# A three-round slot-attention and FFN kernel: the loop over the rounds written out as straight code

## The reference

```
k = ln(ctx) @ wk + bk;  v = ln(ctx) @ wv + bv
slots = q_mu + exp(q_logsig) * layernorm(x)
for _ in range(3):
    q      = ln(slots) @ wq + bq
    attn   = softmax(k @ q.T / scale, over slots) + 1e-8
    attn   = attn / attn.sum(over tokens)
    slots  = (attn.T @ v) @ wu + bu + slots
    slots  = gelu(ln(slots) @ w1 + b1) @ w2 + b2 + slots
    slots  = ln(slots + cond)
x = x + slots
h = layernorm(gelu(layernorm(x) @ ternary(W_fc).T)) * w + b
x = x + h @ ternary(W_proj).T
```

## Time and profile before

| | |
|---|---|
| runs, median of 3 | 343.67 us (343.62 to 344.61) |
| profiled execution | 340.61 us |
| its span | 338.7 us, mean granted TensorE clock 0.995 |
| PE busy | 316.1 us (93%) |
| DVE busy | 294.2 us (87%) |
| ACT busy | 235.9 us (70%) |
| POOL busy | 202.7 us (60%) |

### The profile page before, as it was taken

How to read it: one execution, slowest core, us unless ns; L and a number is a source line. 1 busy time by engine, 2 the same in 40 slices (tenths; PEclk the granted TensorE clock), 3 DMA queues, 4 the chain that set the end, 5 groups by cost and what they waited for, 6 DMA issues and landing times. The chain is left out here.

```text
span 338.7 us, 6940 instructions
## 1 busy us (share of the span) xinstructions
PE 316.1 (93%) x1758; PEld 260.4 (77%) x1758; DVE 294.2 (87%) x851; ACT 235.9 (70%) x563; POOL 202.7 (60%) x385
## 2 busy tenths in 40 slices
PE   8999999999999899799999899799969799999995
PEld 7887888888887778688877788587846577777774
DVE  3699968898899989699999898989898999999874
ACT  2369986968458867386678675656537888888881
POOL 3268965256698763557887636556753965444341
PEclk9999999999999999999999999999998999999999
DMA  7997000000000000000000000000000000000001
GB/s 284 329 344 319 0 1 2 0 0 4 0 2 1 0 3 1 3 1 0 0 1 0 0 0 1 2 0 2 1 0 0 3 31 35 31 29 2 34 31 62
DMA packets 5310, 13.19 MB, mean 39 GB/s; under 512 B 672, under 2 KB 672, under 8 KB 4896
## 3 DMA queue, kind: packets, MB, share of 16 engines
q1 hardware_dynamic: 4160, 10.88, 8.7%
q10 hardware_dynamic: 1120, 1.98, 1.6%
HBM read 10.76 MB, written 2.10 MB: 38 GB/s over the span
## 5 line engine op out<-in xcount | busy, mean ns | idle before, releaser
L293 DVE BATCH_NORM_STATS2 stats<-S 128x6 f32<-128x256 f32 (+1 forms) x112 | 42.1, 417 | 9.4 <-DMA S<-ctx 3.5
L344 PE MATMUL ps_mid<-XT,KT 128*128 128x256 f32 x192 | 46.1, 383 | 3.9 <-ACT XT L360 3.9
L344 PE MATMUL ps_low<-V,PR 128*128 128x257 f32 x192 | 46.4, 384 | 3.5 <-DVE PR L866 3.5
L344 PE MATMUL ps_low<-wn,GT 128*128 128x256 f32 x192 | 46.4, 385 | 1.1 <-ACT GT L642 1.1
L344 PE MATMUL ps_mid<-XT,wt 128*128 128x256 f32 x192 | 45.6, 380 | 0.7 <-ACT XT L360 0.7
L344 PEld LDWEIGHTS ps_low<-V,PR 128*128 128x128 f32 x192 | 35.8, 190 | 10.8 <-DVE PR L866 3.8
L639 ACT ACTIVATE PR<-ps_mid,nmax 128x256 f32<-128x256 f32 x48 | 22.4, 472 | 30.1 <-DVE nmax L876 30.0
L344 PEld LDWEIGHTS ps_low<-wn,GT 128*128 128x128 f32 x192 | 36.8, 194 | 7.1 <-ACT GT L642 2.1
L311 POOL TENSOR_TENSOR lnm_ab<-lnm_mv,mhalf 128x2 f32<-128x2 f32 x24 | 17.3, 721 | 41.5 <-DVE lnm_mv L301 41.5
L344 PEld LDWEIGHTS ps_mid<-XT,KT 128*128 128x128 f32 x192 | 34.6, 190 | 8.9 <-ACT PR L639 4.6
L360 ACT ACTIVATE XT<-ps_t 128x512 f32<-128x512 f32 x56 | 33.2, 592 | 8.6 <-PE ps_t L336 8.6
(11 more groups left out here) (124 smaller groups left out, 704.1 us busy)
## 6 DMA issues: line engine op xcount, KB each, us to landing
S<-ctx SPq DMA_DIRECT2D x8, 256.0 KB, 3.8
X<-x SPq DMA_DIRECT2D x8, 256.0 KB, 3.4
out<-X SPq DMA_DIRECT2D x8, 256.0 KB, 2.0
rowv<-rows SPq DMA_DIRECT2D x1, 1920.0 KB, 9.6
wf<-w_fc_t SPq DMA_DIRECT2D x1, 1024.0 KB, 11.5
wf<-w_proj_t SPq DMA_DIRECT2D x1, 1024.0 KB, 13.5
wt<-w_tr ACTq DMA_DIRECT2D x1, 512.0 KB, 4.3
wn<-w_nat ACTq DMA_DIRECT2D x1, 512.0 KB, 5.4
```

Of the source, the lines that this page charges most:

```text
L293: dve.bn_stats(ln.st[:, at, j, 0:6], tiles[:, j]).then_inc(ln.stats_done, 1)
L344: last = pe.matmul(dst(m), lhs_t[:, c, m * P:(m + 1) * P], rhs[:, c, 0:n], start=(c == 0), stop=(c == 1))
```

## The change

`in_rounds` no longer makes a loop. It calls the step function for t = 0 and t = 1 as plain numbers, so steps 7 to 22 stand twice in each engine's program, with constant semaphore counts and constant addresses. The tests that told the written-out head by `isinstance(t, int)` now ask for `t == 0` (on DVE together with `s < LEAD`). The order of the steps and the operations in them are unchanged, as are the loops of the prologue and of the FFN. The diff, cut:

```diff
-        def in_rounds(eng, step):
+        def in_rounds(step):
             for s in range(LEAD):
                 step(0, s, False)
-            with eng.Fori(0, ROUNDS - 1) as t:
+            for t in range(ROUNDS - 1):
                 for s in range(LEAD, STEPS + LEAD):
                     step(t, s, False)
             for s in range(LEAD, STEPS + LEAD):
...
-                if isinstance(t, int) and not last and s < 2:
+                if t == 0 and not last and s < 2:
                     ln_coef(pool, lni, B - 2 + s, s)
...
-                head = isinstance(t, int) and not last
+                head = t == 0 and s < LEAD and not last
...
-                chunk = None
+                part = None
                 if not head and not last and s < LEAD + B:
-                    k = s - LEAD
-                    chunk = (t * B + k) * CHUNK
-                    chunk_slot[0] = k % 2
-                    cut = bass.ds(chunk, CHUNK)
+                    part = t * B + (s - LEAD)
+                    cut = slice(part * CHUNK, (part + 1) * CHUNK)
...
             def ternary_below(n, cut):
-                dve.tensor_scalar(below[:, chunk_slot[0]], wf[:, cut], thr_now(1, n), None, ALU.is_lt).then_inc(below_ready, 1)
+                dve.tensor_scalar(below[:, n % 2], wf[:, cut], thr[:, 1, n // B:n // B + 1], None, ALU.is_lt)\
+                   .then_inc(below_ready, 1)
...
-            in_rounds(dve, rounds_with_pass)
+            in_rounds(rounds)
```

More of the change, by code:

```diff
@@ L457, in rounds @@
             def rounds(t, s, last):
-                if s == 2 and isinstance(t, int) and not last:
+                if s == 2 and t == 0 and not last:
                     pool.wait_ge(rows_in, 16)
@@ L498, in rounds @@
                     into_ffn(s)
-            in_rounds(pool, rounds)
+            in_rounds(rounds)
             def both(b, u, first, last):
@@ L611, in rounds @@
                     copy_xt(act, ring(r, half, b), b % 2)
-                if s < 2 and isinstance(t, int) and not last:
+                if s < 2 and t == 0 and not last:
                     ln_apply(act, lni, B - 2 + s, s, Y[:, B - 2 + s], XH[:, B - 2 + s], xq_ready)
-                if s in (3, 4) and isinstance(t, int) and not last:
+                if s in (3, 4) and t == 0 and not last:
                     act.wait_ge(ffn_in, 32)
@@ L647, in rounds @@
                     into_ffn(s)
-            in_rounds(act, rounds)
+            in_rounds(rounds)
             def both(b, u, first, last):
@@ L889, in rounds @@
                     ps = ps_low[b % 2]
-                    fold = chunk is not None and at == 0
+                    fold = part is not None and at == 0
                     dve.wait_ge(low_ready, n + 1)
@@ L895, in rounds @@
                         if fold:
-                            ternary_below(t * B + k, cut)
+                            ternary_below(part, cut)
                         dve.wait_ge(cinv_ready, r * B + (b + 1))
@@ L910, in rounds @@
                     if fold:
-                        ternary_above(t * B + k, cut, (t * B + k))
+                        ternary_above(part, cut)
                     bn_sum(dve, ln, r * B + b, b)
@@ L929, in ternary_below, with ternary_above @@
             def ternary_below(n, cut):
-                dve.tensor_scalar(below[:, chunk_slot[0]], wf[:, cut], thr_now(1, n), None, ALU.is_lt).then_inc(below_ready, 1)
-            def ternary_above(n, cut, done):
+                dve.tensor_scalar(below[:, n % 2], wf[:, cut], thr[:, 1, n // B:n // B + 1], None, ALU.is_lt)\
+                   .then_inc(below_ready, 1)
+            def ternary_above(n, cut):
                 dve.wait_ge(below_ready, n + 1)
[L934 to L945, removed]
-            in_rounds(dve, rounds_with_pass)
+                dve.scalar_tensor_tensor(out=w3[:, cut], in0=wf[:, cut], scalar=thr[:, 0, n // B:n // B + 1],
+                                         in1=below[:, n % 2], op0=ALU.is_gt, op1=ALU.subtract).then_inc(tern_ready, 1)
+            in_rounds(rounds)
             def both(b, u, first, last):
@@ L1123, in rounds @@
                         pe.wait_ge(low_read, 2 * n + 2)
-                        if isinstance(t, int) and s == 3 and not last:
+                        if t == 0 and s == 3 and not last:
                             pe.wait_ge(w_fold, FOLD_ALL)
-                        if isinstance(t, int) and s == SUM_STEP and not last:
+                        if t == 0 and s == SUM_STEP and not last:
                             pe.wait_ge(mag_ready, 2)
@@ L1136, in rounds @@
                     into_ffn(s)
-            in_rounds(pe, rounds)
+            in_rounds(rounds)
             def both(b, u, first, last):
```

## The result

The changed kernel takes 338.54 us (338.33 to 339.19, 4 runs) against 343.99 us (343.62 to 344.61, 4 runs) of the kernel before beside it: a ratio of 0.9847, 95% interval 0.9829 to 0.9865, a gain of 5.45 us. Its profiled execution took 339.19 us with a span of 337.3 us, the slowest of the four.

The account below looks back on a forecast made before the run. PE, busy nearly all the time, was taken to bound the kernel. DVE's jump (2.56 us) plus register work (0.74 us) made 3.30 us, off 343.67 us: 340.4 us, with 339.2 to 342.4 us for 8 in 10.

Parts of the forecast that it names:

- The jump back on DVE: Start of the second pass: removing DVE's jump and its 2.81 us hole saves 2.56 us in steps 7 to 18.
- The jumps on PE, ACT and POOL: Those engines' jumps back in the rounds go too, at no gain, since their losses lie under DVE's hole.
- Register instructions: DVE's register work in the loop: four gaps, 0.37 us a pass, come off PE's stall; 0.74 us in two passes.
- they come off that stall one for one: Step 19: closing DVE's register gaps shortens PE's stalls on XT (1.41 and 1.40 us) equally, 0.37 us a pass.
- Nothing behind the loop takes it back: Last round and FFN keep code and order, inputs already loaded, so the whole 3.30 us gain reaches the end.
- The median of the runs is 3.06 us above the profiled execution; I take the same difference off it: Whole kernel: the 3.06 us between median and profiled execution stays, so the gain comes off 343.67 us.
- larger register costs: Rival: both step 19 stalls on XT close wholly, 5.4 us gain, 338.3 us; chance 0.06.
- No hole stands in the FFN's loop: Rival denied here: shifted code brings 2.81 us of DVE back at the FFN's jump, 343.2 us; chance 0.05.
- Straight code fetched too late: Rival: in the second pass three late 8 KB code pieces cost 6.9 us, giving 347 us; chance 0.04.
- no issue wait over 0.3 us: Sign: in the new profile no DVE instruction in the rounds has an "issue" wait of over 0.3 us.

Follow-up runs that it names:

- dve_straight: Kernel before with only DVE's loop over the rounds written out; PE, ACT and POOL keep theirs: 339.66 us, ratio 0.9891.
- pad70: Kernel before, loops kept, with 70 increments of an unused semaphore at the start of DVE's program, shifting its loop's code: 340.54 us, ratio 0.9901.
- base_again: The kernel before once more, unchanged: 343.12 us, ratio 0.9988.
- base_look: One more profiled execution of the unchanged kernel before, taken for its clock: 345.09 us, mean clock 0.979.
- dve_loop: Kernel before with the rounds written out on PE, ACT and POOL; DVE keeps its loop: 343.48 us, ratio 1.0006.
- dve_loop_held: dve_loop plus 7 matmuls without a reader on PE, ahead of the second pass's product that waited for DVE's PR: 343.18 us, ratio 1.0010.
- after_beside: The changed kernel again, unchanged, run beside later variants of it: 338.57 us, ratio 0.9886 of the kernel before.
- after_held: The changed kernel plus 21 matmuls without a reader in PE's waits at the entry into the FFN: 336.80 us, ratio 0.9832 of the kernel before.

## Why the prediction was wrong

*The jump back on DVE*: right. 2.56 us forecast, 2.76 measured in steps 7 to 18 of the second pass, 2.43 of them with DVE's loop alone written out (47.64 us in dve_straight). pad70 confirms the cause, code that has to come again: the same jump without the transfer costs 0.30 us.

*The jumps on PE, ACT and POOL*: put at nothing. True while DVE's hole covers them; behind it they and their register work are worth 0.5 us in the passes (131.30 to 130.79).

*Register instructions*: 0.74 us forecast, off the stall in step 19; 0.51 measured in steps 19 to 22 (0.25 and 0.26 us), 0.33 of it with DVE's loop alone written out. The gaps closed as read, but "they come off that stall one for one" failed: the stalls on XT went to 1.2 us and not to 1.0, since the first two threshold tests became 0.13 and 0.14 us longer.

*"Nothing behind the loop takes it back"*: this step failed, in both directions. The last round gives another 0.80 us. The row for it stood in the trace of before, the sum at 240.45 with 0.51 us of idle time put down to DVE's own statistics. I had looked for "issue" alone. The pause and the longer PR are in all five profiled kernels of three rounds in which DVE's code has its old place (before, base_again, base_look, dve_loop, dve_loop_held; last round 49.6 to 49.7 us) and in none of the seven in which it is shifted or straight (48.8 to 48.9 us). That it is code coming late is argued from this, not shown. The FFN takes 2.1 us back in the profiled execution, and some 1 us at the mean clock of before (87.0 against 86.0, after_beside), because the fall of the clock now lies behind PE's waits and not ahead of them; the start takes back 0.44 us. The profiled execution was to go to 337.3 us and took 339.19: it gained 1.42 us, not 3.30.

*"The median of the runs is 3.06 us above the profiled execution; I take the same difference off it"*: this step failed too, the other way and by more, and it decides that the forecast came out too small. Beside the changed kernel the median of before was 3.38 us above its profiled execution (343.99 less 340.61); the median of the changed kernel is 0.65 us below its own (338.54 against 339.19). So of the 5.45 us 1.42 are the gain from profile to profile, and 4.03 are this difference, which I had taken for a constant. That 340.4 us came as near as it did is in part luck, two errors against each other: 1.9 us too much gain in the profile, 3.7 us too much difference kept.

What stood in the difference is known in part. 57 of the 70 recorded executions of before ran at a lower mean clock than the profiled one, and the two profiles of that kind (base_look, and dve_loop_held with the same DVE program) show further falls of the clock, which make the FFN 2.9 and 1.4 us longer. The changed kernel has them less often (6 of 16) and pays less for them: 339.19 us at 0.988 to 0.989 against 338.36 at 0.995, where the kernel before goes from 341.12 to 343.31. At 0.995 and more the gain is 341.12 - 338.36 = 2.76 us, less than the 3.97 of the passes and the last round, as the table has it: start and FFN take some of it back. At 0.988 to 0.990 it is 343.31 - 339.19 = 4.12 us; that this is near 3.97 is chance, since the FFN differs there as well. The only profile of the kind with DVE's old code, dve_loop_held at 342.48 us, lies 0.8 us below that 343.31, and for these 0.8 us there is no profile.

*The rivals.* The nearest in time, 338.3 us by larger register costs, had the wrong cause. No hole stands in the FFN's loop. Straight code fetched too late did not show: my sign "no issue wait over 0.3 us" failed by its letter (0.84 us), but that addition starts as PE's product ends.

*What stays open*: why the clock falls twice at the entry into the FFN more often in the kernel before. PE's wait there is longer in it (2.75 against 1.97 us), but pad70, with 1.98 us, had a clock of 0.66 right behind it. And whether the fall behind the stall at 143 us, seen once, makes the slowest 15 executions: dve_loop_held had none of them in 12, which is too few to tell. No execution of before at a clock of 1.00 was profiled; they were no faster (340.67 to 341.31 us) than those at 0.995, as one would expect if the first fall of before costs next to nothing.

## What to carry to other kernels

Where a loop's timeline has one long "issue" hole at its jump back, price it by the same steps in the pass without a jump, and try a shift of the code before writing the loop out. Before an "issue" wait is put down to code, see whether one of the instruction's inputs ended just ahead of it. Before a saving is taken off the median, ask in which clock the profiled execution ran and in which the runs did, and where in the span the clock fell: a fall ahead of a wait can cost nothing, and one behind it is paid for. Where an engine pauses on its own earlier instruction, compare that piece with the same piece elsewhere; and keep PE busy through short waits ahead of a stretch that it bounds.

## What the runs showed of the hardware

- A jump back on DVE whose target has to come again cost 2.74 to 2.93 us, in all eight jumps of six profiles with DVE's loop in its old place; a shift by 70 instructions took it to 0.30 us.
- In the straight code of the changed kernel's rounds DVE has two waits of over 0.25 us that the profile puts down to "issue" (0.28 and 0.84 us), and both end 0.10 us behind a product of PE. The Trainium skill, Runtime: NRT & Kernel Launch, section Instruction fetch mechanics, says that fetching of straight code is hidden behind execution; the trace of these rounds agrees. Of the pause of 0.51 us at 240.45 us in the kernel before the cause is open.
- At a mean clock of 0.995 the FFN took 86.0 us where the fall lay ahead of PE's waits (before) and 87.0 us where it lay behind them (after_beside), against 85.8 us without a fall (after_held).
- 21 products that nobody reads, put into waits of PE of 1.97, 1.36, 0.48 and 1.15 us, held its granted clock at 1.00 behind them and gained 1.77 us.
